# Block rounds of a two-layer decoder: the reciprocal of the denominators made from an integer guess and ScalarE's logarithm and exponential

## The reference, cut to what matters

```
x = x + L0_attn(layernorm(x))          # linear attention
x = x + wkv(w, u, k=layernorm(x), v=context)
x = x + mixture_of_experts(layernorm(x))   # 8 experts, top 2
x = layer_1(x)

# wkv, one step, without the running maximum o that only keeps exp in range
y = (p + exp(u + k_t) * v_t) / (q + exp(u + k_t))
p = exp(w) * p + exp(k_t) * v_t
q = exp(w) * q + exp(k_t)
```

## Time and profile before

| | us |
|---|---|
| median of three runs | 3060.1 |
| lowest, highest run | 3059.43, 3067.85 |
| the profiled execution's own time | 3064.77 |
| its span in the trace | 3063.0 |
| mean granted TensorE clock over the span | 0.951 |

### The profile page before, as it was taken

One profiled execution on the slowest core, in us unless ns is written; L12 is line 12 of the kernel. 1 busy time (PEld: TensorE's weight loads), 2 busy tenths in 40 slices (PEclk: granted clock), 3 DMA queues, 4 the chain that ended last, 5 costly groups with the idle time before them and its releaser, 6 DMA issues. The chain is left out here.

```text
span 3063.0 us, 68267 instructions
## 1 busy us (share of the span) xinstructions
PE 2760.3 (90%) x22128; PEld 2307.7 (75%) x22128; DVE 2565.5 (84%) x5547; ACT 1954.2 (64%) x4120; POOL 2126.1 (69%) x2651
## 2 busy tenths in 40 slices
PE   6999999999999999999788499558899999999978
PEld 3888888888888888888455399436777777777767
DVE  6888888888888888888499577488999999999973
ACT  5888778788787878878344155345656565565642
POOL 5897666666666666666378455288888888888870
PEclk9999999999999999999899699768999999999999
DMA  4564344444344444443444599300000000000000
GB/s 144 172 206 161 130 151 130 149 133 150 128 130 145 142 138 142 147 138 112 139 152 145 190 334 336 132 14 19 17 27 19 27 19 25 21 24 22 20 5 11
DMA packets 186021, 340.09 MB, mean 111 GB/s; under 512 B 40810, under 2 KB 104179, under 8 KB 179075
## 3 DMA queue, kind: packets, MB, share of 16 engines
q1 hardware_dynamic: 179586, 319.55, 31.8%
q0 software_dynamic: 6144, 16.79, 1.8%
HBM read 264.67 MB, written 63.18 MB: 107 GB/s over the span
## 5 line engine op out<-in xcount | busy, mean ns | idle before, releaser
L1802 POOL TENSOR_TENSOR l_prod<-l_sco,l_kv 128x256 f32<-128x256 f32 x512 | 380.4, 783 | 43.3 <-DVE l_sco L2316 43.3
L1795 POOL TENSOR_TENSOR l_prod<-l_q,l_kv 128x256 f32<-128x256 f32 x512 | 358.6, 742 | 57.8 <-DVE l_att L2324 57.8
L718 DVE SCALAR_TENSOR_TENSOR a_cq<-a_PQ,a_taps,a_cq 128x504 f32<-128x504 f32 (+2 forms) x384 | 281.8, 734 | 75.9 <-ACT a_cq L584 66.8
L718 DVE SCALAR_TENSOR_TENSOR a_ck<-a_PK,a_taps,a_ck 128x504 f32<-128x504 f32 (+2 forms) x384 | 280.7, 731 | 9.6 <-ACT a_ck L584 0.3
L342 POOL TENSOR_TENSOR a_tq<-a_cq,a_tq 128x512 f32<-128x512 f32 x128 | 166.0, 1297 | 130.8 <-ACT a_tq L590 130.4
L329 POOL TENSOR_TENSOR a_hrs<-a_hve,a_neghalf 128x8 f32<-128x8 f32 x128 | 209.7, 1638 | 25.2 <-DVE a_hve L735 25.2
L485 PE MATMUL a_Y<-a_wo,a_og_parts 128*128 128x256 f32 x1536 | 207.2, 285 | 4.5 <-POOL a_og_parts L336 4.5
L412 PEld LDWEIGHTS a_X<-a_wv,a_xb 128*128 128x128 f32 x1536 | 199.9, 188 | 12.1 <-issue 1.2
L412 PE MATMUL a_PQ<-a_x_hi,a_wqk 128*128 (+1 forms) x512 | 196.2, 424 | 12.6 <-issue 11.9
L342 POOL TENSOR_TENSOR a_tk<-a_ck,a_tk 128x512 f32<-128x512 f32 x128 | 163.7, 1279 | 62.6 <-ACT a_tk L590 62.6
L412 PE MATMUL a_X<-a_wv,a_xb 128*128 128x256 f32 x1536 | 204.1, 282 | 0.8 <-DMA a_xb<-a_x_lo 0.8
(11 more groups left out here) (400 smaller groups left out, 8488.7 us busy)
## 6 DMA issues: line engine op xcount, KB each, us to landing
a_wqk<-qk_parts SPq DMA_DIRECT2D x112, 512.0 KB, 3.3
m_wgu<-gate_up_parts SPq DMA_DIRECT2D x39, 1024.0 KB, 7.5
a_wv<-v_parts SPq DMA_DIRECT2D x56, 512.0 KB, 3.7
a_wg<-g_parts SPq DMA_DIRECT2D x112, 256.0 KB, 3.3
a_wo<-o_parts SPq DMA_DIRECT2D x112, 256.0 KB, 2.9
a_dr<-decays SPq DMA_DIRECT2D x256, 64.0 KB, 2.5
m_hs<-sorted_rows SPq DMA_DIRECT2D x39, 256.0 KB, 6.5
sorted_outs<-m_ys SPq DMA_DIRECT2D x39, 256.0 KB, 6.8
```

The lines of the kernel that those rows point to most:

```text
L718: nc.vector.scalar_tensor_tensor(out=acc, in0=src, scalar=taps[p][:, tap + k:tap + k + 1], in1=acc, op0=ALU.mult, op1=ALU.add).then_inc(s_ ...
L1795: nc.gpsimd.tensor_tensor(out=prod[:, h], in0=qv[:, h:h + 1, :].to_broadcast([P, H, HD]), in1=kk, op=ALU.mult).then_inc(S("E_pqk"), 1)
L1802: nc.gpsimd.tensor_tensor(out=prod[:, h], in0=sco[:, h:h + 1, :].to_broadcast([P, HD, H]), in1=vv, op=ALU.mult).then_inc(S("E_pav"), 1)
```

## The change

In `reciprocal(y)` DVE no longer takes the reciprocal. It makes `near`, a guess of 1/den, by arithmetic on the bits (an integer multiply by -1 and an add of a constant), then `den = den * near`, a number near one. ACT then takes the logarithm of that and the exponential of its negative, which is the reciprocal of the number near one; this stands on ACT between `k_out(f)` and `h_out(r)`. In `quotient(y)` DVE multiplies `num` first by `near`, then, as before, by `den`. A tile `near` of 128x1024 is added, and ACT's table set is named ahead of the first exponential: one that has both functions.

```
+                def reciprocal(b):                                   # ACT
+                    act.wait_ge(S("left"), b + 1)
+                    nc.scalar.activation(den[:], den[:], ACT.Ln).then_inc(S("log"), 1)
+                    act.wait_ge(S("log"), b + 1)
+                    nc.scalar.activation(den[:], den[:], ACT.Exp, scale=-1.0).then_inc(S("rec"), 1)
...
+                nc.scalar.preload_act_table_set("natural_log_exp_and_others")
                 act.wait_ge(S("tab"), 5)
                 nc.scalar.activation(keep[:, :, 1:SEG], keep[:, :, 1:SEG], ACT.Exp).then_inc(S("keep"), 1)
...
                     if f is not None:
                         k_out(f)
+                    if y is not None:
+                        reciprocal(y)
                     if r is not None:
                         h_out(r)
...
                 def reciprocal(b):                                   # DVE
                     dve.wait_ge(S("den"), b + 1)
-                    nc.vector.reciprocal(den[:], den[:]).then_inc(S("rec"), 1)
+                    nc.vector.tensor_scalar(near[:].bitcast(I32), den[:].bitcast(I32), -1.0, INVERSE_BITS, ALU.mult, ALU.add).then_inc(S("near"), 1)
+                    dve.wait_ge(S("near"), b + 1)
+                    nc.vector.tensor_tensor(out=den[:], in0=den[:], in1=near[:], op=ALU.mult).then_inc(S("left"), 1)

                 def quotient(b):
+                    dve.wait_ge(S("num"), b + 1)
+                    nc.vector.tensor_tensor(out=num[:], in0=num[:], in1=near[:], op=ALU.mult).then_inc(S("scaled"), 1)
+                    dve.wait_ge(S("scaled"), b + 1)
                     dve.wait_ge(S("rec"), b + 1)
-                    dve.wait_ge(S("num"), b + 1)
                     nc.vector.tensor_tensor(out=num[:], in0=num[:], in1=den[:], op=ALU.mult).then_inc(S("y"), 1)
```

More of the change, by code:

```diff
@@ L796, in recurrence_and_experts @@
     BOUND = 60.0
+    I32, INVERSE_BITS = mybir.dt.int32, float(0x7EF311C0)
     SEG = SEQ + 1
@@ L851, in recurrence_and_experts @@
             pp, qp = own("pp", [P, NS, SEG]), own("qp", [P, NS, SEG])
-            den, num = own("den", [P, NS, SEQ]), own("num", [P, NS, SEQ])
+            den, num, near = own("den", [P, NS, SEQ]), own("num", [P, NS, SEQ]), own("near", [P, NS, SEQ])
             keep, eh, ev = (own(n, [P, NS, SEG]) for n in ("keep", "eh", "ev"))
```

## The result

The changed kernel took 3083.4 us (median of five runs, 3079.56 to 3083.77) against 3065.6 us of the kernel before on the same chip (five runs): a ratio of 1.006, with a 95% interval of 1.0045 to 1.0074. It is slower by 17.8 us; forecast were 16.6, as 3077 us against a median of 3060.1, in a range of 3067 to 3089. The three runs of before that the forecast started from had a median 5.5 us lower than the five.

What follows compares the result with a forecast made beforehand. The prediction took the loop through TensorE's router, not VectorE's reciprocal, to bound the rounds. Added costs in rounds 2 to 8 summed to 16.65 us, so 3060.1 + 16.6 = 3076.7, rounded to 3077, range 3067 to 3089.

Steps and rivals of the forecast that it cites:

- What bounds the rounds: Block rounds: VectorE idles before choose until TensorE's router ends, 0.29 to 2.54 us, so the reciprocal isn't in the loop.
- The loop as read: Rounds: choose, quotient, place, sent_to, statistics, GpSimd's power, xn, kvs copy, v_T, k_T, h_T, hb, router, choose again.
- Part 1: Reciprocal leaves VectorE: 6.52 us eight times, only lengthening the wait before choose in rounds 2 to 8; gain nothing.
- Part 2: near (0.8 us) and left (1.22 us, after waiting for num) on VectorE: costs nothing, covered by the freed reciprocal time.
- Part 3: Logarithm and exponential before hb on ScalarE: 2.07 us; router late by 1.1 us, 1.57 in rounds 5 and 7.
- Part 4: Second product in quotient, between choose and place, inside the loop: 1.25 us in each of seven rounds.
- Part 5: Giving back: te waits for down_low anyway in rounds 3 and 4, leaving 0.7 of 1.1 us; round 5 saves nothing.
- Part 6: Round 1, no choose: quotient waits for the exponential, 3.4 us later, but xn is held by ScalarE's queue; 0, bound 1.
- Part 7: Table loads on ScalarE: a possible load of 1.28 us before the expert loop's first tanh is hidden; cost 0.
- the reciprocal on the path: Rival: VectorE's work bounds the rounds, each of eight nets 3.25 us less, 26 us faster, 3034; chance 0.06.
- The absorbed case: Rival: v_T stays warm in rounds 3, 4, 6 and down_low doesn't move; cost 9 us or below; chance 0.14.
- The harder one: Rival: left loses to num and ev, v_T goes cold in rounds 2, 5, 7; 27.6 us, 3088; chance 0.12.

Runs made afterwards that it cites:

- both costs moved out of the loop: Changed kernel with the product num * near moved ahead of choose and ScalarE's logarithm and exponential moved behind hb: 3069.7 us, ratio 1.0015.
- the short filler: Changed kernel with filler products of 128x512 on TensorE, one ahead of the router and two ahead of the rank counts: 3081.9 us, ratio 1.0068.
- before and the product: Kernel before with a product of num with a tile of ones added in front of quotient's own: 3074.3 us, ratio 1.0041.
- two versions with early work for the next block: Statistics a round early, in changed kernel with product and pair moved: 3073.1 us; power ahead of scatters, weights_low behind reciprocal, in kernel before: 3071.7 us.

## Why the prediction was right or wrong

**What bounds the rounds: right.** The reciprocal was not in the loop. Every `choose` of rounds 2 to 8 is released by the router after the change too, and VectorE waits 5.1 to 8.3 us before it instead of 0.3 to 2.5. With both costs moved out of the loop, the missing reciprocal gained nothing. The loop as read holds too: `xn` starts 4.4 us behind `sent_to` in every round from 3 to 7, before and changed.

**Part 1, gain of nothing: right**, by the same run. Its limits became visible: where `quotient` was put ahead of `choose`, or the statistics, the reciprocal came on the path.

**Part 2, near and left: right but for round 8.** `near` took 0.67 us (0.8 taken), `left` 3.08 us by the trace (about 2 forecast), behind GpSimd's `num` as said (which had itself waited for `near`, 2.49 us instead of 2.18), and in rounds 1 to 7 ScalarE did not wait for it. `left` never lost to `ev` too: in round 2 `ev` was ready when `num` ended and took 3.17 us, behind `left`; from round 3 on it waits for ScalarE's `eh` and starts later. By the rule of the Trainium skill (SBUF — State Buffer, "SBUF: two separate sides") the two engines block each other for a whole instruction, and the trace agrees: 3.08 us beside 1.22. "Part 2 costs nothing" took as cover that ScalarE is busy with `fk` until `left` is done. Round 8 has no `fk`, and there the logarithm waited 1.54 us for `left`, which `residual`'s wait of 2.01 us had pushed back; with the short filler, where `residual` waited 0.58 us, the logarithm did not wait.

**Part 3, the pair: right in its price, not round by round.** The logarithm took 1.05 us, the exponential 1.06. In round 6 `hb` starts 2.95 us behind the start of `fk` instead of 0.92, so 2.03 us late as forecast. What of it reaches the router was 7.64 us over rounds 3 to 8 by the slacks (1.1 us in rounds 3, 4 and 6); it was 9.62, round by round -0.17, 2.39, 2.33, -0.08, 2.21 and 2.94. A router that starts no later although `hb` does was the prediction's own sign against part 3. In rounds 3 and 6 it came, but not because the pair was free: `v_T` ran at the upper level there, and the pair used up the 1.7 us that this gave. The 6.8 us of the sum against 6.9 (taken away) and 8.3 (added) are close partly by luck, as the last column of the table of rounds 3 to 8 shows.

**Part 4, the product: right.** 7.5 us in these rounds by the sum, 7.8 and 8.3 measured, with the same reserve; two products of 1.22 us stand one behind the other.

**Part 5: right in round 3, in round 4 only in size.** They grew by 1.66 and 2.24 against 1.95. In round 3 `down_low` came 0.47 us later and still set the pace, as forecast. In round 4 `choose` came 3.06 us later and behind `down_low`, so the whole stall of 2.62 us was saved; the slower clock at `k_T` and the router had used it up. In round 5 the stall went to `te` (2.98 us) and not to a product of `quotient`.

**Part 6: not quite.** VectorE did wait 6.29 us for the exponential in round 1, but the next `xn` was no longer held by ScalarE's own queue: it started 0.60 us later by the ruler, after 1.32 us of idle time that GpSimd ended, where the forecast took 0 (bound 1). Round 1 is taken together with round 2, 2.60 against 2.35. This stretch differs between kernels by 2 us in ways that don't follow the edits (before and the product has 61.3 us, the kernel before 62.9), so it proves little.

**Part 7, the tables: right.** One more load, of 1.28 us, stands right before the first tanh, which still waited 1.72 us behind it, as against 2.92. No table was loaded in a round. ScalarE in the changed kernel:

```profile
1768.16 1.28 ACT L1354 ACT_TABLE_LOAD   x1
...
1771.16 0.63 ACT L1354 ACTIVATE m_th<-m_gp 128x512 f32<-128x512 f32 x1 [1.72 <-DVE m_gp L1585]
```

**What was missed: 3.8 us of 20.4.** The sum left out the clock and put it in two rivals, as a `v_T` going cold or warm. `v_T` did go warm in rounds 3 and 6, which saved 3.35 us up to `h_T` and hid part of the cost. The clock went down behind the router, at `cross_kv`, and reached the path by `y_T` and `residual` in rounds 5, 7 and 8, as read from the trace of the changed kernel; the short filler took most of these waits away and gave back 0.76 and 1.08 us in rounds 5 and 8, but lost as much at `v_T` and `k_T`. What the clock costs as such stays open. Of the 2.8 us that remain in rounds 3 to 8 with both parts moved, a part lies in rounds 3 and 5, where `v_T` is slower (1.94 and 1.59 us against 1.40 and 1.07 before) and `h_T` starts 1.20 and 1.66 us later, and a part in round 8, where `xh` starts 0.68 us later, released by GpSimd; whether that is GpSimd's later `ev` was not tried apart.

The rivals: the reciprocal on the path is refuted. The absorbed case did not occur, though `v_T` went warm in two of its three rounds. The harder one had 11 us above the forecast; about 3.8 came, by neither of its two ways: `left` never lost to `ev`, and `v_T` was cold in none of rounds 2, 5 and 7. In the total, the nearness of 17.8 to 16.6 owes something to luck: the rounds grew by 20.4 us, and the profiled executions made up 1.0 us behind them; the totals vary by more than that.

## What to carry to other kernels

An engine that sits idle before an instruction of another engine's making has slack, and taking its longest instruction away moves only where it waits; read the idle time behind an instruction before its duration. When work is replaced by several smaller pieces, it is their places in the queues that cost: here about 2 us of ScalarE ahead of a copy and 1.2 us of VectorE behind a wait made 17 us, and the same instructions at another place cost little (1.1 us by the rounds, 0.6 to 8 by the totals). Shortening one loop of a balanced pipeline (five tries here) brought up the next one, VectorE's own work or GpSimd's queue, at the same length or a worse one. And a sum that comes out right round by round should still be held against the trace step by step: two of these rounds had the forecast length by other terms than the forecast ones.

## What the runs showed that was not expected

- A scatter issued by GpSimd takes 0.96 us, but 2.99 us beside VectorE's first scan, and powers of 128x4 elements 1.0 to 2.2 us. The later these fall in a round, the more of them meets the scans. In two versions with early work for the next block (246.8 and 245.8 us) it is this queue that `xh` waits for; no run took the queue apart to show that it made them slow.
- A cast of 128x8 elements on VectorE can cost 2.58 us, a product of 128x64 3.12, when GpSimd's 2.35 us subtraction has just begun. What is cut ahead of such a place counts only as far as GpSimd's instruction itself comes earlier: with `quotient` ahead, `down_low` of round 4 ended at 1606.14 us and `sent_to` at 1606.19.
- The multiply and add on int32 of 128x1024 elements took 0.67 us, about half of a product of the same size (1.22).
- Holding TensorE's clock up in one place by filler was followed by a cold start in another: with the short filler `cross_kv` and router were mostly at 1.98 and 1.95 us, and `v_T` in rounds 3 and 6 at 1.94 instead of 1.07.
